# Scores of the local layers in three products instead of four, the mix next to them, and another order of all stages

## The chip, the cores and the metric

One core of one Trainium2 chip. The metric is the device time of one execution in microseconds (us). Three runs of the kernel before took 3424.27, 3425.03 and 3427.98 us; the median is 3425.03. The profile is of one further execution.

## The reference, cut to what matters

A batch of 32 sequences of 128 tokens with 128 features passes four blocks: a cross attention, six local transformer layers, a second cross attention, and a quantised linear layer. The change is in the six local layers only. One layer computes, for 16 heads of width 64:

```python
q, k, v = split(x @ Wqkv)                      # 128 -> 3 * 1024
q = rotary(l2norm(q) * q_scale);  k = rotary(l2norm(k) * k_scale)
# windows of 32 queries; each sees its own 32 keys and the 32 before them
sim  = einsum('bhwie,bhwje->bhwij', bq, bk2) * 8        # masked: later keys, more than 32 back, padding
out  = einsum('bhwij,bhwje->bhwie', softmax(sim), bv2)
x = out @ Wo + x
x = (a * gelu(gate)) @ W2 + b2 + x             # a, gate = split(layernorm(x) @ W1 + b1), width 341 each
```

In front of both halves of a layer the upper 64 features are shifted by one token. All of this is in float32.

## The kernel before, in words

`local_layers` (from line 553 on) writes out the instruction streams of TensorE (`pe`), ScalarE (`act`), VectorE (`dve`), GpSimd (`pool`) and SyncE (`sp`, DMA issues only) by hand. A unit `u` is one sequence in one layer; there are 6 * 32 = 192. Each engine runs a loop over `step`, and in every step it does a fixed list of stages, each for unit `step - lag`; the list and the lags are the order of that engine. Stages that are called `closing` run once in four steps, for a group of four sequences, and `second` ones once in two. The engines are tied by semaphores; an engine does its list strictly in order, so a stage whose input is late holds up everything behind it in the list.

The stages of a unit are, on TensorE: `project` (L732, three times: q, k and v, each two products of 128x512), `transpose_qk` (L742, eight 128x128 transposes each for q and k), `scores` (L759), `mix` (L786), every second step `project_out` (L800), and every fourth step `mlp_mean` (L809), three `mlp_up` (L827), `mlp_variance` (L817) and `mlp_down` (L838). ScalarE squares q and k (L896), takes the reciprocal norms (L905, L907), copies the transposed q and k (`copy_qk`, L914), v (L889) and the mix (L928) out of PSUM and does the exponentials and the gelu, which need different tables. VectorE makes the rotary products (L1026, L1027), the sums of squares (L1034), the mask, the maxima and sums of the softmax and a block transpose of the probabilities. GpSimd does the rest of the rotation (L1154), the normalisation (L1162) and two passes over the probabilities. The transposed probabilities go to DRAM and back (`store_probs`, `place_probs`), and half of v is moved between partitions by DMA (`place_v`).

Each float32 product stands in the profile as two weight loads and two matmuls, which are called records below. A product that needs only a part of the 128x128 array is given a tile of it, by `tile_position` and the size of its operands. In `scores`, for each of the eight pairs of heads (`t`), there are four windows of 32 queries and two heads (`j`, in the upper and the lower 64 rows): 8 products whose weights are 64 rows by 32 columns (64*32 in the profile), with 64 keys moving. That makes 64 products and 128 records for a unit. In `mix` all products have weights of 64*64, and there are 48 products (96 records) for a unit. All the other stages use the whole array (128*128, or 128*85 and 85*128 in the last tile of the MLP).

PSUM is used as four pairs of banks in rotation. The order in which TensorE's stages take them is `ROTATING`, which has to match TensorE's list, and a stage waits until the pair it takes has been read out (`banks.fill`).

Of the kernel before, what the change touches and what calls it, by code (L numbers as in the profile page):

```python
# [17 lines left out]
NB, S, D = 32, 128, 128  # L18
GB = 4
# [6 lines left out]
DEPTH, HD, WIN = 6, 64, 32  # L26
# [19 lines left out]
NEAR = 2 * WIN  # L46
# [72 lines left out]
def build(nc, dram):  # L119
    stack = ExitStack()  # L120
    with stack:
# [34 lines left out]
        def phase_end(engine):  # L156
            engine.drain().then_inc(phase_over, 1)
# [395 lines left out]
        def local_layers(phase):  # L553
            here = ExitStack()
            with here:
# [39 lines left out]
                for n in ("squared", "producted", "summed", "rotations", "normalised", "turned", "copied"))  # L595
# [10 lines left out]
                sem("up_made"), sem("gelu_made"), sem("hidden_made"), sem("down_made"), sem("y_ready"))  # L606

            LAST = 14
            ROTATING = (("q", 0, 1), ("up2", 13, GB), ("mix", 6, 1), ("k", 0, 1), ("v", 4, 1), ("scores", 2, 1), ("out", 6, 2),
                        ("up0", 11, GB), ("mean", 7, GB), ("up1", 11, GB), ("variance", 10, GB), ("down", 13, GB), ("kT", 1, 1),  # L610
                        ("qT", 1, 1))
            pair_of, turn = {}, 0
            for step in range(UNITS + LAST):
                for stage, lag, every in ROTATING:
                    u = step - lag
# [82 lines left out]
            def sp(sp):  # L698
                for step in range(UNITS + LAST):
                    place_probs(step - 5, sp)  # L700
                    layer, into = step // NB, step % NB
                    if layer < DEPTH - 1 and into == NB - 1:
                        load_qk(sp, layer + 1, 1)
                    if 0 < layer < DEPTH and into == 3:
                        load_v(sp, layer)
                    place_v(step - 4, sp)
                    if layer < DEPTH - 1 and into == NB - 2:
                        load_qk(sp, layer + 1, 0)
                    if 0 < layer < DEPTH and into == 5:
                        load_out(sp, layer)  # L710
                    if 0 < layer < DEPTH and into == 12:
                        load_mlp(sp, layer)
                    store_probs(step - 4, sp)
                sp.wait_ge(probs_placed, P_PLACED * UNITS)

            def pe(pe):
# [29 lines left out]
                @each(UNITS)  # L746
                def scores(u):
                    i = pair_of["scores", u]
                    banks.fill(pe, i, (masked, u + 1))
                    pe.wait_ge(copied[0], u + 1)  # L750
                    pe.wait_ge(copied[1], u + 1)
                    for t in range(IT):
                        for window in range(S // WIN):
                            these = slice(window * WIN, (window + 1) * WIN)
                            near = slice(max(window - 1, 0) * WIN, max(window + 1, 2) * WIN)
                            for j in range(2):
                                rows = slice(HD * j, HD * j + HD)
                                at = j * BANK + t * NEAR
                                mm = pe.matmul(  # L759
                                    pairs[i][these, at:at + NEAR], qkT[u % 2][rows, 0, t, these],  # L760
                                    qkT[u % 2][rows, 1, t, near], start=True, stop=True,
                                    tile_position=(rows.start, these.start))
                    mm.then_inc(scored, 1)

                @each(UNITS)
# [74 lines left out]
                    mm.then_inc(down_made, 1)  # L840

                for step in range(UNITS + LAST):
                    project(step, 0)
                    mlp_up(step - 13, 2)
                    mix(step - 6)
                    project(step, 1)
                    project(step - 4, 2)
                    scores(step - 2)
                    project_out(step - 6)
                    mlp_up(step - 11, 0)  # L850
                    mlp_mean(step - 7)
                    mlp_up(step - 11, 1)
                    mlp_variance(step - 10)
                    mlp_down(step - 13)
                    transpose_qk(step - 1, 1)
                    transpose_qk(step - 1, 0)
                phase_end(pe)

            def act(act):
# [122 lines left out]

                for step in range(-1, UNITS + LAST):
                    square(step, 0)
                    reciprocal_norms(step - 1)
                    mlp_gelu(step - 13, 2)
                    mlp_affine(step - 11)
                    mlp_shift(step - 7)
                    square(step, 1)
                    copy_mix(step - 6)  # L990
                    copy_v(step - 4)
                    exponentials(step - 4)
                    prepare(step + 1)
                    mlp_log(step - 10)
                    mlp_root(step - 10)
                    mlp_gelu(step - 11, 0)
                    mlp_gelu(step - 11, 1)
                    mlp_square(step - 9)
                    copy_qk(step - 1, 1)
                    copy_qk(step - 1, 0)  # L1000
                phase_end(act)

            def dve(dve):
# [108 lines left out]
                for step in range(UNITS + LAST):  # L1112
                    if step < UNITS and step % NB == 0:
                        start_layer(step // NB)
                    products(step, 0)
                    turn_probs(step - 5)
                    mlp_hidden(step - 13, 2)
                    products(step, 1)
                    mask_scores(step - 2)
                    sum_squares(step, 0)  # L1120
                    mlp_centre(step - 7)
                    add_out(step - 6)
                    mlp_hidden(step - 11, 0)
                    add_down(step - 13)
                    sum_squares(step, 1)
                    mlp_hidden(step - 11, 1)
                    row_sums(step - 4)
                    clamp_norms(step)
                    row_maxima(step - 2)
                phase_end(dve)  # L1130

            def pool(pool):
                phase_gate(pool, phase)
                for t in (*xs, mlp_xs):
                    pool.memset(t[P // 2:, :, 0:1], 0.0).then_inc(zeroed, 1)

                @each(UNITS)
                def lower(u):
                    pool.wait_ge(maxed, u + 1)
                    pool.tensor_tensor(probs[u % 3][:, :, :], probs[u % 3][:, :, :],  # L1140
                                       negmax[u % 2][:, :].unsqueeze(2).broadcast_to([P, H, NEAR]), ALU.add).then_inc(lowered, 1)

                @each(UNITS)
                def normalise_probs(u):
                    pool.wait_ge(inverted, u + 1)
                    pool.tensor_tensor(probs[u % 3][:, :, :], probs[u % 3][:, :, :],  # L1146
                                       rowsum[u % 2][:, :].unsqueeze(2).broadcast_to([P, H, NEAR]), ALU.mult).then_inc(probs_normed, 1)

                @each(UNITS)
                def rotate(u, part):  # L1150
                    pool.wait_ge(producted[part], u + 1)
                    if u >= 2:
                        pool.wait_ge(turned[part], u - 1)
                    pool.tensor_tensor(rotated[u % 2][:, part].rearrange("p h (s d) -> p s h d", s=2),  # L1154
                                       halves(times_cos[part][:, :]), halves(times_sin[part][:, :]), ALU.add).then_inc(rotations[part], 1)

                @each(UNITS)
                def normalise(u, part):
                    rt = rotated[u % 2][:, part]
                    pool.wait_ge(rnormed, u + 1)  # L1160
                    pool.wait_ge(rotations[part], u + 1)
                    pool.tensor_tensor(rt, rt, rnorm[u % 2][:, part * H:(part + 1) * H].unsqueeze(2).broadcast_to([P, H, HD]),  # L1162
                                       ALU.mult).then_inc(normalised[part], 1)

                @each(UNITS)
                @closing
                def mlp_scale(g):
                    pool.wait_ge(rooted, g + 1)
                    pool.tensor_tensor(centred[:, :], centred[:, :], spread[:, :], ALU.mult).then_inc(scaled, 1)

                for step in range(UNITS + LAST):
                    rotate(step - 1, 1)
                    normalise(step - 1, 1)
                    normalise(step - 1, 0)
                    lower(step - 3)
                    rotate(step, 0)
                    mlp_scale(step - 10)
                    normalise_probs(step - 4)
                phase_end(pool)

            return load_first, sp, pe, act, dve, pool
# [718 lines left out]
```

## Time and profile before

| | |
|---|---|
| median of three runs | 3425.03 us |
| the profiled execution | 3413.21 us, of it span 3411.4 us |
| first attention, until the local layers begin | 0 to about 243 us |
| local layers | about 243 to 3090 us |
| TensorE busy, share of the span | 3245.9 us, 95% |
| VectorE busy | 2943.4 us, 86% |
| GpSimd busy | 2639.8 us, 77% |
| ScalarE busy | 2379.1 us, 70% |
| mean granted TensorE clock | 0.982 of full speed |

"Busy" is the time in which at least one instruction of the engine is under way. The profile shows weight loads (PEld) apart from matmuls (PE); a load normally runs while the matmul before it streams. The start times are what the text reads from; the ends of matmuls are modelled.

### The profile page before, as it was taken

The numbers are of one execution on the slowest core, as the hardware profiler recorded it, in microseconds if no ns is written. First come the engines' busy times: TensorE is split into PE (matmuls) and PEld (weight loads), VectorE is DVE, ScalarE is ACT, GpSimd is POOL, SyncE is SP. The second block draws the span as 40 slices with busy tenths as digits, with TensorE's granted clock in tenths as the row PEclk, the third lists the DMA queues.
The fourth block names the chain that finished last, engine by engine and source line by source line (L and its number), as shares of the span: only waits on it lengthen the run. The fifth ranks groups of instructions, "written<-read, shape, count | busy, mean of one in ns | idle before, by whom it ended". The sixth has DMA issues, their size and how long they took to land.

```text
span 3411.4 us, 130897 instructions
## 1 busy us (share of the span) xinstructions
PE 3245.9 (95%) x56355; PEld 2054.7 (60%) x56386; DVE 2943.4 (86%) x3343; ACT 2379.1 (70%) x4288; POOL 2639.8 (77%) x1408
## 2 busy tenths in 40 slices
PE   7977999999999999999999999999999999977996
PEld 4545666666666666666666666666666666643554
DVE  6869989889999999998989898898999999935887
ACT  6865677667676767676776776776767676746885
POOL 1229988888888888888888888888888888833576
PEclk9989999999999999999999999999999999988998
DMA  2002333443433344334433334343344333330000
GB/s 94 2 1 64 122 113 111 120 126 114 120 112 112 117 126 119 113 108 126 125 113 117 112 110 123 119 120 113 113 125 125 118 111 112 110 123 1 2 11 17
DMA packets 229188, 336.05 MB, mean 99 GB/s; under 512 B 39046, under 2 KB 151044, under 8 KB 228228
## 3 DMA queue, kind: packets, MB, share of 16 engines
q1 hardware_dynamic: 228612, 327.68, 31.7%
q8 instruction: 446, 7.31, 0.9%
q14 instruction: 130, 1.06, 0.1%
HBM read 124.14 MB, written 102.76 MB: 67 GB/s over the span
## 4 chain that ended last, share of the span: by engine, by line
PE 84%; issue 5%; POOL 4%; ACT 3%; DVE 3%; SPq 0%; DMA 0%; POOLq 0%; DVEq 0%; ACTq 0%
PE psum L732 29%; PE psum L800 10%; PE psum L742 9%; PE psum L786 8%; PE psum L759 8%; PE psum L827 7%; PE psum L838 4%; POOL f_rotated L1154 2%; ACT x_expo L1480 1%; PE psum L817 1%; PE psum L809 1%; ACT x_expo L391 1%; PE psum L1337 1%; PE psum L1347 1%; PE psum L309 1%
## 5 line engine op out<-in xcount | busy, mean ns | idle before, releaser
L732 PE MATMUL psum<-w_qkv,f_xs 128*128 128x512 f32 x2304 | 1081.2, 606 | 18.9 <-issue 14.2
L1154 POOL TENSOR_TENSOR f_rotated<-f_times_cos,f_times_sin 128x1024 f32<-128x1024 f32 x384 | 908.7, 2367 | 9.3 <-DVE f_times_sin L1027 9.3
L1162 POOL TENSOR_TENSOR f_rotated<-f_rotated,f_rnorm 128x1024 f32<-128x1024 f32 x384 | 722.6, 1903 | 38.2 <-ACT f_rnorm L907 11.9
L732 PEld LDWEIGHTS psum<-w_qkv,f_xs 128*128 128x128 f32 x2304 | 410.1, 191 | 402.4 <-issue 393.6
L896 ACT ACTIVATE f_squares<-psum 128x1024 f32<-128x1024 f32 x384 | 392.9, 1023 | 361.4 <-PE psum L732 356.4
L1146 POOL TENSOR_TENSOR f_probs<-f_probs,f_rowsum 128x1024 f32<-128x1024 f32 x192 | 365.2, 1902 | 329.1 <-DVE f_rowsum L1066 329.1
L1026 DVE TENSOR_TENSOR f_times_cos<-psum,rot 128x1024 f32<-128x1024 f32 x384 | 469.8, 1223 | 131.6 <-ACT f_squares L896 127.8
L914 ACT COPY f_qkT<-psum 128x1024 f32<-128x1024 f32 x384 | 369.9, 1013 | 210.8 <-PE psum L742 210.7
L1027 DVE TENSOR_TENSOR f_times_sin<-psum,rot 128x1024 f32<-128x1024 f32 x384 | 466.1, 1214 | 0.0
L1034 DVE TENSOR_REDUCE f_sumsq<-f_squares 128x16 f32<-128x1024 f32 x384 | 463.4, 1209 | 0.0
L742 PEld LDWEIGHTS psum<-consts,f_rotated 128*128 128x128 f32 x3072 | 348.5, 141 | 98.0 <-issue 89.2
L742 PE MATMUL psum<-consts,f_rotated 128*128 128x128 f32 x3072 | 371.1, 274 | 17.7 <-POOL f_rotated L1162 14.7
L1140 POOL TENSOR_TENSOR f_probs<-f_probs,f_negmax 128x1024 f32<-128x1024 f32 x192 | 365.2, 1902 | 0.0
L786 PEld LDWEIGHTS psum<-f_probsT,f_v 64*64 64x64 f32 x6144 | 262.9, 135 | 163.1 <-issue 163.1
L800 PE MATMUL psum<-f_outT,w_o 128*128 128x256 f32 x1536 | 358.6, 387 | 1.2 <-ACT f_outT L928 1.2
L759 PEld LDWEIGHTS psum<-f_qkT 64*32 64x32 f32 x24576 | 254.2, 105 | 146.9 <-issue 145.3
L786 PE MATMUL psum<-f_probsT,f_v 64*64 64x64 f32 (+1 forms) x6144 | 310.1, 228 | 15.8 <-issue 15.8
L800 PEld LDWEIGHTS psum<-f_outT,w_o 128*128 128x128 f32 x1536 | 285.1, 190 | 45.5 <-issue 1.8
L786 PE MATMUL psum<-f_probsT,f_v_moved 64*64 64x32 f32 (+1 forms) x12288 | 307.5, 217 | 0.0
L827 PE MATMUL psum<-f_xn,w 128*128 128x512 f32 (+1 forms) x576 | 281.2, 612 | 7.7 <-ACT f_xn L970 7.7
L759 PE MATMUL psum<-f_qkT 64*32 64x64 f32 x24576 | 285.4, 225 | 0.8 <-issue 0.8
L786 PEld LDWEIGHTS psum<-f_probsT,f_v_moved 64*64 64x64 f32 x12288 | 286.2, 136 | 0.0
(175 smaller groups left out, 5159.5 us busy)
## 6 DMA issues: line engine op xcount, KB each, us to landing
f_v_moved<-f_v SPq DMA_DIRECT2D x768, 128.0 KB, 2.8
turned_blocks<-w_qkv SPq DMA_DIRECT2D x192, 512.0 KB, 3.0
f_probsT<-turned_blocks SPq DMA_DIRECT2D x768, 128.0 KB, 2.8
w_qkv<-in_l_wqkv SPq DMA_DIRECT2D x18, 512.0 KB, 4.0
w_o<-in_l_wo SPq DMA_DIRECT2D x6, 512.0 KB, 4.6
w_qkv<-in_ctxT SPq DMA_DIRECT2D x1, 2048.0 KB, 8.7
out<-x_f_result SPq DMA_DIRECT2D x8, 256.0 KB, 2.2
w<-in_l_w SPq DMA_DIRECT2D x6, 341.0 KB
```

Of the source, the lines that this page charges most:

```text
L732: mm = pe.matmul(pairs[i][:, j * BANK:(j + 1) * BANK], xs[g % 2][:, u % GB, :], w_qkv[:, part * INNER + j * BANK:part * INNER + (j + 1) * ...
L742: tr = pe.transpose(pairs[i][:, t * S:(t + 1) * S], rotated[u % 2][:, part, 2 * t:2 * t + 2, :].rearrange("p h d -> p (h d)"), ident)
L759: mm = pe.matmul(pairs[i][these, at:at + NEAR], qkT[u % 2][rows, 0, t, these], qkT[u % 2][rows, 1, t, near], start=True, stop=True, tile_p ...
L786: mm = pe.matmul(pairs[i][cols, at + windows.start * WIN:at + windows.stop * WIN], values, probsT[u % 2][rows, windows, j, :], start=True, ...
L800: mm = pe.matmul(pairs[i][:, 0:GT // 2], w_o[:, t, :], outT[:, t, tokens], start=t == 0, stop=t == IT - 1)
L827: mm = pe.matmul(pairs[i][0:n, a * BANK:a * BANK + GT], w_1[:, a * FF + o:a * FF + o + n], xn[:, :], start=True, stop=True)
L896: act.activation(squares[part][:, :], pair("qk"[part], u), ACT.Square).then_inc(squared[part], 1)
L1026: dve.tensor_tensor(halves(times_cos[part][:, :]), halves(taken), table(0), ALU.mult)
L1027: dve.tensor_tensor(halves(times_sin[part][:, :]), halves(taken)[:, ::-1], table(1), ALU.mult).then_inc(producted[part], 1)
L1034: dve.tensor_reduce(sumsq[u % 2][:, part * H:(part + 1) * H], squares[part][:, :].rearrange("p (s h d) -> p h s d", s=2, h=H), axis=XY, op ...
L1154: pool.tensor_tensor(rotated[u % 2][:, part].rearrange("p h (s d) -> p s h d", s=2), halves(times_cos[part][:, :]), halves(times_sin[part] ...
L1162: pool.tensor_tensor(rt, rt, rnorm[u % 2][:, part * H:(part + 1) * H].unsqueeze(2).broadcast_to([P, H, HD]), ALU.mult).then_inc(normalised ...
```

## The change

Three edits, all in `local_layers`. First, in `scores` the first two windows of a head become one product: 64 queries (weights of 64*64) by the first 64 keys, which are the keys that both windows look at. The other two windows stay as they are (64*32). So there are three products for a head instead of four, 48 in a unit, and 96 records. They are issued pair of heads by pair of heads: two of 64*64, then four of 64*32, then the next pair.

Second, on TensorE `mix` comes directly behind `scores`.

Third, the lists of all engines are in another order, with other lags of v (3 instead of 4), of the exponentials and row sums (3 instead of 4), of lowering by the maxima (2 instead of 3), and of parts of the MLP; `ROTATING` follows.

```diff
-                        for window in range(S // WIN):
-                            these = slice(window * WIN, (window + 1) * WIN)
-                            near = slice(max(window - 1, 0) * WIN, max(window + 1, 2) * WIN)
+                        for these, near in ((slice(0, 2 * WIN), slice(0, 2 * WIN)), (slice(2 * WIN, 3 * WIN), slice(WIN, 3 * WIN)),
+                                            (slice(3 * WIN, 4 * WIN), slice(2 * WIN, 4 * WIN))):
                             for j in range(2):
...
 TensorE:
                 for step in range(UNITS + LAST):
+                    mlp_mean(step - 9)
                     project(step, 0)
-                    mlp_up(step - 13, 2)
+                    mlp_up(step - 12, 2)
+                    scores(step - 2)
                     mix(step - 6)
                     project(step, 1)
-                    project(step - 4, 2)
-                    scores(step - 2)
+                    mlp_up(step - 11, 0)
+                    project(step - 3, 2)
+                    mlp_up(step - 11, 1)
                     project_out(step - 6)
-                    mlp_up(step - 11, 0)
-                    mlp_mean(step - 7)
-                    mlp_up(step - 11, 1)
-                    mlp_variance(step - 10)
                     mlp_down(step - 13)
+                    transpose_qk(step - 1, 0)
                     transpose_qk(step - 1, 1)
-                    transpose_qk(step - 1, 0)
+                    mlp_variance(step - 9)
 ScalarE, after:
                     square(step, 0); mlp_gelu(step - 12, 2); reciprocal_norms(step - 1); copy_mix(step - 6); square(step, 1)
                     exponentials(step - 3); mlp_gelu(step - 11, 0); mlp_affine(step - 10); prepare(step + 1)
                     mlp_square(step - 9); copy_v(step - 3); mlp_gelu(step - 11, 1); copy_qk(step - 1, 0)
                     copy_qk(step - 1, 1); mlp_shift(step - 7); mlp_log(step - 9); mlp_root(step - 9)
 VectorE, after:
                     turn_probs(step - 5); products(step, 0); mlp_hidden(step - 12, 2); sum_squares(step, 0)
                     mask_scores(step - 2); products(step, 1); sum_squares(step, 1); mlp_hidden(step - 11, 0)
                     add_down(step - 13); row_sums(step - 3); add_out(step - 6); mlp_hidden(step - 11, 1)
                     row_maxima(step - 2); mlp_centre(step - 8); clamp_norms(step)
 GpSimd, after:
                     normalise(step - 1, 0); normalise(step - 1, 1); rotate(step, 0); normalise_probs(step - 4)
                     rotate(step, 1); lower(step - 2); mlp_scale(step - 9)
 SyncE:
-                    if 0 < layer < DEPTH and into == 3:
+                    if 0 < layer < DEPTH and into == 2:
                         load_v(sp, layer)
-                    place_v(step - 4, sp)
+                    place_v(step - 3, sp)
```

## Rows read from the trace of the kernel before

**Rows 1.** The page, part 1: busy time and share of each engine.
```profile
PE 3245.9 (95%) x56355; PEld 2054.7 (60%) x56386; DVE 2943.4 (86%) x3343; ACT 2379.1 (70%) x4288; POOL 2639.8 (77%) x1408
```

**Rows 2.** The page, part 4: the chain that ended last, by engine.
```profile
PE 84%; issue 5%; POOL 4%; ACT 3%; DVE 3%; SPq 0%; DMA 0%; POOLq 0%; DVEq 0%; ACTq 0%
```

**Rows 3.** Busy time of each engine in four steps of layer 4.
```profile
core 0: us, PE busy (x) PEld busy (x) DVE busy (x) ACT busy (x) POOL busy (x), PEclk, DMA share, GB/s
1697.13:1754.44 57.31, 57.31 (x1070) 36.63 (x1076) 51.81 (x56) 40.65 (x52) 49.96 (x26) 1.00 0.37 112
```

**Rows 4.** The chain of waits from 1690 to 1760 us: start, duration, what.
```profile
1697.13 1.41 PE psum L759 x91
...
1703.03 1.75 PE psum L742 x16
1704.78 1.72 PE psum L732 x4
1706.50 1.53 PE psum L786 x96
1708.03 3.63 PE psum L732 x8
1711.66 1.42 PE psum L759 x91
...
1754.44 1.42 PE psum L759 x91
```

**Rows 5.** Line 759 between 1705.95 and 1713.2 us: count, shortest/median/longest ns.
```profile
L759 PEld LDWEIGHTS psum<-f_qkT x128: 102/106/107, 1711.6 to 1712.8; 64*32 64x32 f32 x128
L759 PE MATMUL psum<-f_qkT x128: 213/216/240, 1711.6 to 1712.9; 64*32 64x64 f32 x128
```

**Rows 6.** Weight loads around one mix: start us, us, what [idle before].
```profile
1705.05 0.19 PEld L732 LDWEIGHTS psum<-w_qkv,f_xs 128*128 128x128 f32 x1 [0.24 <-issue]
1705.48 0.19 PEld L732 LDWEIGHTS psum<-w_qkv,f_xs 128*128 128x128 f32 x1 [0.24 <-issue]
1706.43 0.13 PEld L786 LDWEIGHTS psum<-f_probsT,f_v 64*64 64x64 f32 x1 [0.76 <-issue]
1706.43 0.13 PEld L786 LDWEIGHTS psum<-f_probsT,f_v_moved 64*64 64x64 f32 x1
1706.44 0.13 PEld L786 LDWEIGHTS psum<-f_probsT,f_v 64*64 64x64 f32 x1
1706.45 0.13 PEld L786 LDWEIGHTS psum<-f_probsT,f_v_moved 64*64 64x64 f32 x1
...
1707.78 0.14 PEld L786 LDWEIGHTS psum<-f_probsT,f_v 64*64 64x64 f32 x1
1707.96 0.30 PEld L732 LDWEIGHTS psum<-w_qkv,f_xs 128*128 128x128 f32 x2
1708.50 0.19 PEld L732 LDWEIGHTS psum<-w_qkv,f_xs 128*128 128x128 f32 x1 [0.24 <-issue]
```

**Rows 7.** Weight loads in the first attention, 118 to 122 us.
```profile
118.14 0.11 PEld L302 LDWEIGHTS psum<-mask_past,ident_bf 128*128 128x128 bf16 x2
118.68 0.97 PEld L309 LDWEIGHTS psum<-x_queries,x_keys 32*128 32x128 f32 x16 [0.42 <-issue]
119.77 0.30 PEld L253 LDWEIGHTS psum<-xres,mean_mat 128*128 128x128 f32 x2
120.83 0.81 PEld L319 LDWEIGHTS psum<-x_expo,x_vpad 128*32 128x32 f32 x32 [0.76 <-issue]
```

**Rows 8.** Transposes, their copies and the q projection behind them, in order of time.
```profile
1716.57 1.91 PE L742 MATMUL psum<-consts,f_rotated 128*128 128x128 f32 x16
1717.64 1.93 ACT L914 COPY f_qkT<-psum 128x1024 f32<-128x1024 f32 x2 [2.75 <-PE psum L742]
1718.31 1.88 PE L732 MATMUL psum<-w_qkv,f_xs 128*128 128x512 f32 x4
```

**Rows 9.** The chain of waits where TensorE takes over, at a layer's start, and after the last q.
```profile
397.46 1.06 PE psum L742 x8
...
1598.95 2.96 issue
1601.91 3.00 PE psum L732 x4
...
2998.49 2.51 issue
```

More of the change, by code:

```diff
@@ L608, in local_layers @@
             LAST = 14
-            ROTATING = (("q", 0, 1), ("up2", 13, GB), ("mix", 6, 1), ("k", 0, 1), ("v", 4, 1), ("scores", 2, 1), ("out", 6, 2),
-                        ("up0", 11, GB), ("mean", 7, GB), ("up1", 11, GB), ("variance", 10, GB), ("down", 13, GB), ("kT", 1, 1),
-                        ("qT", 1, 1))
+            ROTATING = (("mean", 9, GB), ("q", 0, 1), ("up2", 12, GB), ("scores", 2, 1), ("mix", 6, 1), ("k", 0, 1), ("up0", 11, GB),
+                        ("v", 3, 1), ("up1", 11, GB), ("out", 6, 2), ("down", 13, GB), ("qT", 1, 1), ("kT", 1, 1), ("variance", 9, GB))
             pair_of, turn = {}, 0
@@ L758, in scores @@
                                 at = j * BANK + t * NEAR
[L759 to L762, printed above, removed]
+                                mm = pe.matmul(pairs[i][these, at:at + NEAR], qkT[u % 2][rows, 0, t, these],
+                                               qkT[u % 2][rows, 1, t, near], start=True, stop=True,
+                                               tile_position=(rows.start, these.start))
                     mm.then_inc(scored, 1)
@@ L984, in act @@
                     square(step, 0)
+                    mlp_gelu(step - 12, 2)
                     reciprocal_norms(step - 1)
-                    mlp_gelu(step - 13, 2)
-                    mlp_affine(step - 11)
-                    mlp_shift(step - 7)
[L989 to L1000, printed above, removed]
+                    copy_mix(step - 6)
+                    square(step, 1)
+                    exponentials(step - 3)
+                    mlp_gelu(step - 11, 0)
+                    mlp_affine(step - 10)
+                    prepare(step + 1)
+                    mlp_square(step - 9)
+                    copy_v(step - 3)
+                    mlp_gelu(step - 11, 1)
+                    copy_qk(step - 1, 0)
+                    copy_qk(step - 1, 1)
+                    mlp_shift(step - 7)
+                    mlp_log(step - 9)
+                    mlp_root(step - 9)
                 phase_end(act)
@@ L1114, in dve @@
                         start_layer(step // NB)
+                    turn_probs(step - 5)
                     products(step, 0)
-                    turn_probs(step - 5)
-                    mlp_hidden(step - 13, 2)
+                    mlp_hidden(step - 12, 2)
+                    sum_squares(step, 0)
+                    mask_scores(step - 2)
                     products(step, 1)
[L1119 to L1122, printed above, removed]
+                    sum_squares(step, 1)
                     mlp_hidden(step - 11, 0)
                     add_down(step - 13)
-                    sum_squares(step, 1)
+                    row_sums(step - 3)
+                    add_out(step - 6)
                     mlp_hidden(step - 11, 1)
-                    row_sums(step - 4)
+                    row_maxima(step - 2)
+                    mlp_centre(step - 8)
                     clamp_norms(step)
-                    row_maxima(step - 2)
                 phase_end(dve)
@@ L1171, in pool @@
                 for step in range(UNITS + LAST):
-                    rotate(step - 1, 1)
+                    normalise(step - 1, 0)
                     normalise(step - 1, 1)
-                    normalise(step - 1, 0)
-                    lower(step - 3)
                     rotate(step, 0)
-                    mlp_scale(step - 10)
                     normalise_probs(step - 4)
+                    rotate(step, 1)
+                    lower(step - 2)
+                    mlp_scale(step - 9)
                 phase_end(pool)
```

## The prediction

> **What bounds the kernel now.** I read the page's busy shares first: TensorE is at work for 95% of the span, VectorE for 86%, GpSimd for 77% [rows 1]. The chain that ended last, which is where a shorter instruction shortens the run, lies on TensorE for 84% of the span [rows 2]. Then the windows view over four steps of a layer: 57.31 us, of which TensorE is busy for 57.31, VectorE 51.81, GpSimd 49.96 and ScalarE 40.65, with the clock granted in full [rows 3]. So a step takes 14.33 us and TensorE never rests; if it were faster, the next floors would be VectorE at 51.81 / 4 = 12.95 us a step and GpSimd at 12.49. The chain view of the same stretch says what a step is made of: transposes 1.75, q 1.72, mix 1.53, k and v 3.63, scores 1.42, and one MLP or output stage, here 3.65 [rows 4]. The reader is to see that each piece begins where the last one ends. The chain is of this kind from 398.5 us, where GpSimd stops being the last, to 2998.5 us; in between lie five starts of a layer, where it shows a wait of 2.96 us and a slow first q of 3.00 instead of 1.72, some 5 us each with what follows [rows 9]. (2600 - 25) / 14.33 = 180 steps are set by TensorE, and each is worth what TensorE gains or loses in it.
>
> **What a change of tile costs on TensorE.** This decides the case, so I read it from the weight loads. Inside a run of full-array products a load starts 0.43 us after the one before (1705.05, 1705.48), as soon as the earlier matmul begins to stream: it is hidden. The next load, the first of `mix` with 64*64, would be due at 1705.91. It starts at 1706.43, that is when the last full product, begun at 1705.91 and streaming 0.43, has ended, and 0.09 later [rows 6]. Within `mix` four tiles load at 1706.43 to .45, about 7 ns apart, beside each other. On the way out the last load is at 1707.78 and the first full one only at 1707.96, and its product streams only when that load is through, 0.30 - 0.19 = 0.11 us later [rows 6]. The first attention shows the same with rows alone cut (128*128 to 32*128: the two full loads are over at 118.25, and the next, at 118.68, has waited 0.42 us for their products) and with columns alone cut (128*128 to 128*32: second stream from 119.77 + 0.11 + 0.43 = 120.31 to 120.74, load at 120.83, 0.09 later) [rows 7]. So each change of the tile's shape that this trace has empties the array: about 0.09 us after the last stream, and then a weight load that nothing hides. It has no change between two cut shapes, and the new `scores` makes fifteen of them in a unit: 64*64, 64*32, 64*64, and so on through the eight pairs of heads.
>
> The Trainium skill, "TensorEngine Tiling (Array Packing)", Tiling Modes, says that changing the tiling mode, and not just the tile, drains TensorE. The rows above agree for changes from and to the full array; for 64*64 to 64*32 no row shows it. By the page my forecast holds, and without it the first rival would be as good.
>
> **Part 1, three products for a head.** Removed: 128 - 96 = 32 records in a unit. Now 128 records take 1.42 us [rows 4, 5], 11.1 ns each. If only their number counts, 96 take 1.07 and the unit gains 0.35 us. If each change of shape empties the array, a pair of heads takes two legs, one after the other:
> - 64*64, two tiles side by side, two records in each. A full load and a full stream of 128 columns take 1.75 / 16 = 0.109 us [rows 4], so 64 columns take 0.053. Load 0.053, two streams 0.107, empty 0.09: 0.25 us.
> - 64*32, four tiles, two records in each: load 0.027, two streams 0.107, the last tile's first record six places behind (at 7 to 11 ns, 0.04 to 0.07), empty 0.09: 0.26 to 0.29 us.
>
> Together 0.51 to 0.54 us, times eight 4.1 to 4.3; I take 4.2. Against 1.42 that is +2.78 us a step. Ends for this unknown: below, no emptying, 1.07 (-0.35); above, every leg waits for the whole recorded matmul of 0.216 us [rows 5] in place of its stream, 0.32 + 0.37 a pair, 5.5 us (+4.1). I stand near the lower part of the emptying case because the three changes seen all give 0.09 to 0.10 after the stream, not after the record.
>
> **Part 2, mix behind scores.** Two q or k and v stages between cut shapes show the price of a visit to the full array: k and v together take 3.63 us between `mix` and `scores`, where four records take 1.72 and eight would take 3.44 [rows 4]. The 0.19 is the exposed load of 0.11 and the emptying of 0.09. One such visit goes away in each step: -0.19. The change from 64*32 to the 64*64 of `mix` stays, and its emptying is in the last leg above. If the array does not empty there, the gain is the same to within 0.1 us.
>
> **Part 3, the order and the lags.** No instruction is added or taken; they move.
> - `scores` had q, mix, k and v between it and the transposes (1.72 + 1.53 + 3.63); now in the leanest steps only q. The two copies of the transposes end at 1717.64 + 1.93 = 1719.57, and TensorE would reach `scores` at 1718.31 + 1.72 = 1720.03 [rows 8]. Some 0.4 us is left, so I cost it at nothing. If ScalarE comes late by more, everything on TensorE is late by the rest, since `mix` and k are queued behind.
> - `mix` comes 1.42 us or so later after `turn_probs` and the DRAM round trip than before, which helps. v is made and moved one step earlier: `place_v`, four DMAs on SyncE's queue, stands before `store_probs` as before, with one more step until `mix`. `load_v` moves with it. Both at nothing, covered by a whole step; uncovered, a DMA's landing would cost some us once a layer.
> - `mlp_centre` now waits on VectorE for `mlp_mean` at the head of TensorE's next step, once in four steps. Behind it stand `clamp_norms` and the next `turn_probs`; ScalarE needs the clamped sums only behind its square of the next q, which itself needs 1.72 us of TensorE. Nothing. In the same way `mlp_log` on ScalarE and `mlp_scale` on GpSimd wait for a variance at TensorE's step end; behind them stand a square that waits for q in any case, and `normalise`. Nothing.
> - `lower` follows `row_maxima` in the same step instead of the next. VectorE has 14.33 - 12.95 and GpSimd 14.33 - 12.49 us of slack a step [rows 3], and more if TensorE gets longer. Bounds for the whole order: -0.1 us a step (nothing on TensorE stalls now, so hardly below nothing) and +1.4, VectorE's whole slack turned into a stall.
>
> **The sum.** 14.33 + 2.78 - 0.19 = 16.92 us a step; 2.59 * 180 = +466 us. Span 3411.4 + 466 = 3877, execution +1.8 = 3879. The profiled execution of before lies 11.8 us below the median of its runs; with that, 3891 us.
>
> **The rivals.**
> - *Faster: no emptying between the two cut shapes.* They need not conflict, since 64*64 sits in the first 64 columns and the two 64*32 in the last 64, and tiles of one shape do run beside each other [rows 6]. Against it: a full load does run ahead of a full product on the very same cells, so what holds the load back at each change is not that the cells are in use, but the change. Then a step gains 0.35 + 0.19 = 0.54, 180 * 0.54 = 97: 3328 us. If the 96 records go at the pace of `mix`, 1.53 / 96 = 15.9 ns [rows 4], `scores` takes 1.53 and the whole gives 0.08 a step, 14 us: 3411. It is decided at an internal change costing (0.35 + 0.19) / 15 = 0.04 us: above that the kernel is slower. 0.04 is less than half of the 0.09 alone.
> - *Half an emptying.* Between two cut shapes the array may be empty in half the time, 0.045 us, with the next load partly beside it: legs of 0.20 and 0.22, `scores` 3.4, +1.79 a step, +322: 3747 us. The way out of `mix` speaks against it, where the first full load is as late as after a full product.
> - *No emptying, and the order is late.* `scores` stands 0.4 us behind its input, VectorE 0.8 us a step from its floor. A stall of 0.5 to 0.8 us a step takes back the 0.54: 3420 to 3470 us.
>
> **How the numbers follow.** Full emptying 0.60, with 3800 to 3980 us as its own range (legs shorter by the overlap of a load, or 0.4 us more a step from each engine's waits and the emptying at 0.12); half or less, 3500 to 3800, 0.08; above 3980, 0.03; no emptying 0.24, between 3320 and 3411; late order 0.05. The likeliest is 3891. To leave out no more than 2 in 10 the range has to reach over to the fast case: 3325 to 3980. A measurement of this kernel tells a change from none at about 0.2%, 7 us. Slower by more: 0.60 + 0.08 + 0.03 + 0.04 of the late order = 0.75, less 0.03 for small costs in the case between: 0.72. Faster 0.24, within 0.2% 0.04.
>
> **What the profile after would show.** If I am right: line 759 has 18432 matmuls, its time in the chain is about 4.2 us a step, the weight loads in it show a pause before each leg, VectorE's share falls to about 76%, and TensorE's idle time in front of 759's loads grows by over 2 us a unit. If the rival is right: 759 takes 1.1 us in the chain, a step 13.8 us, VectorE at 94%. In both, the full-array stages should show 0.19 less between cut shapes. A chain that leaves TensorE in the steady steps, for ScalarE's copies above all, would show that the order is the cause. Wrong would be: one record rate throughout line 759 without pauses.

## The result and the profile after

The changed kernel takes 3834.28 us (median of 4 runs, 3832.24 to 3840.2) against 3424.65 us for the kernel before (median of 4): a ratio of 1.12, with a 95% interval of 1.1183 to 1.1217. It is 12% slower. The forecast was 3891 us. Its range of 3325 to 3980 reached over to a faster kernel; 3800 to 3980 was the part of it for full emptying at every change. The profiled execution took 3832.62 us, its span 3830.8, so 419.4 us more than the 3411.4 of before.

The page, parts 1 and 4, and from part 5 the group of the scores (now line 757; 731 is the projections, 741 the transposes, 783 `mix`, 797 the output projection, 824 and 835 the MLP):

```profile
PE 3705.9 (97%) x50211; PEld 2352.0 (61%) x50242; DVE 2934.8 (77%) x3343; ACT 2271.0 (59%) x4196; POOL 2641.5 (69%) x1408
...
PE 89%; issue 4%; DVE 3%; ACT 3%; POOL 1%; SPq 0%; DMA 0%; POOLq 0%; DVEq 0%; ACTq 0%
PE psum L731 26%; PE psum L757 20%; PE psum L741 9%; PE psum L797 9%; PE psum L783 8%; PE psum L824 6%; PE psum L835 3%; ACT x_expo L1477 1%; PE psum L814 1%; PE psum L806 1%; ACT x_expo L391 1%; PE psum L1334 1%; PE psum L1344 1%; PE psum L309 1%; DVE x_negmax L472 1%
...
L757 PE MATMUL psum<-f_qkT 64*32 64x64 f32 (+1 forms) x18432 | 793.0, 233 | 1.5 <-ACT f_qkT L911 1.4
```

Against [rows 1] VectorE's and GpSimd's busy time has not changed (2934.8 and 2641.5 us), only their share of a longer span. TensorE has 6,144 matmuls fewer and is busy for 460 us more. The scores were 8% of the chain and are 20%.

Four steps of the middle of a layer, windows view and chain of waits (start, duration, what), which answer to [rows 3] and [rows 4]:

```profile
1909.09:1976.19 67.10, 67.10 (x936) 42.89 (x938) 52.01 (x55) 38.34 (x49) 49.98 (x26) 1.00 0.34 103
```

```profile
1905.62 1.75 PE psum L741 x16
1907.37 1.72 PE psum L731 x4
1909.09 4.06 PE psum L757 x96
1913.15 1.53 PE psum L783 x96
1914.68 1.92 PE psum L731 x4
...
1936.15 3.45 PE psum L797 x16
1939.60 1.75 PE psum L741 x16
...
1976.19 4.06 PE psum L757 x96
```

A step is 67.10 / 4 = 16.78 us where it was 14.33, at the same full clock, and TensorE still never rests. The scores take 4.06 us instead of 1.42: +2.64. `mix` is 1.53 as before. The output projection, which came directly behind the scores in [rows 4], now stands between full stages and takes 3.45 instead of 3.65. 2.64 - 0.19 = 2.45 a step.

The scores of one unit, shortest/median/longest ns (answers to [rows 5]), and two slices of 0.05 us, one from each of two successive legs, of line 757 alone (columns: PE, then PEld, busy and count, granted clock, DMA share, GB/s):

```profile
L757 PEld LDWEIGHTS psum<-f_qkT x96: 102/106/133, 1909.0 to 1912.9; 64*32 64x32 f32 x64, 64*64 64x64 f32 x32
L757 PE MATMUL psum<-f_qkT x96: 215/229/268, 1909.0 to 1912.9; 64*32 64x64 f32 x64, 64*64 64x64 f32 x32
```

```profile
1927.31:1927.36 0.05, 0.05 (x8) 0.00 (x0) 1.00 0.60 246
...
1927.56:1927.61 0.05, 0.05 (x4) 0.00 (x0) 1.00 0.80 328
```

A single record is as short as before. What has grown is the distance: in each leg of about 0.25 us there is a slice with matmuls in flight and no weight load at all. The shares of busy time hide this, since records of 0.22 us bridge the pauses; the number of records and the length of the stage show it.

### The profile page after: what moved, and what is told of

Read it like the earlier page. It is cut to its first block, busy times and chain, and to the rows that moved or that the text cites. A ratio compares the mean times of both kernels' runs of the same rounds, so it can differ in the third digit from the quotient of the medians.

```text
span 3830.8 us, 118517 instructions
## 1 busy us (share of the span) xinstructions
PE 3705.9 (97%) x50211; PEld 2352.0 (61%) x50242; DVE 2934.8 (77%) x3343; ACT 2271.0 (59%) x4196; POOL 2641.5 (69%) x1408
## 4 chain that ended last, share of the span: by engine, by line
PE 89%; issue 4%; DVE 3%; ACT 3%; POOL 1%; SPq 0%; DMA 0%; POOLq 0%; DVEq 0%; ACTq 0%
PE psum L731 26%; PE psum L757 20%; PE psum L741 9%; PE psum L797 9%; PE psum L783 8%; PE psum L824 6%; PE psum L835 3%; ACT x_expo L1477 1%; PE psum L814 1%; PE psum L806 1%; ACT x_expo L391 1%; PE psum L1334 1%; PE psum L1344 1%; PE psum L309 1%; DVE x_negmax L472 1%
## 5 line engine op out<-in xcount | busy, mean ns | idle before, releaser
L757 PE MATMUL psum<-f_qkT 64*32 64x64 f32 (+1 forms) x18432 | 793.0, 233 | 1.5 <-ACT f_qkT L911 1.4
L757 PEld LDWEIGHTS psum<-f_qkT 64*32 64x32 f32 (+1 forms) x18432 | 536.5, 113 | 374.4 <-issue 147.9
L925 ACT COPY f_outT<-psum 128x1024 f32<-128x1024 f32 x192 | 194.3, 1012 | 759.5 <-PE psum L783 759.5
L797 PEld LDWEIGHTS psum<-f_outT,w_o 128*128 128x128 f32 x1536 | 295.0, 192 | 82.8 <-issue 46.2
```

Of the source, the lines that this page charges most:

```text
L757: mm = pe.matmul(pairs[i][these, at:at + NEAR], qkT[u % 2][rows, 0, t, these], qkT[u % 2][rows, 1, t, near], start=True, stop=True, tile_p ...
L797: mm = pe.matmul(pairs[i][:, 0:GT // 2], w_o[:, t, :], outT[:, t, tokens], start=t == 0, stop=t == IT - 1)
```

## Experiments

Ratios are to the kernel before on the same chip, with 95% intervals; before ran there at 3415 to 3417 us (beside the changed kernel: 3424.65).

### The products alone

```diff
 # kernel before, its order kept; in scores:
-                        for window in range(S // WIN):
-                            these = slice(window * WIN, (window + 1) * WIN)
-                            near = slice(max(window - 1, 0) * WIN, max(window + 1, 2) * WIN)
+                        for these, near in ((slice(0, 2 * WIN), slice(0, 2 * WIN)), (slice(2 * WIN, 3 * WIN), slice(WIN, 3 * WIN)),
+                                            (slice(3 * WIN, 4 * WIN), slice(2 * WIN, 4 * WIN))):
```

> The kernel before with only the scores changed to three products a head; order and lags of before. Emptying theory: scores take 4.06 us as in the changed kernel, +2.64 a step, 180 steps +475, less up to 25 us at the layer starts: 3875 to 3900 us (ratio 1.13 to 1.14). Rival (the order is to blame for the loss): under 3500 us.

Measured: 3889.41 us, ratio 1.1388 (1.1366 to 1.1409). A scores stage begins at 2005.87 and the next stage at 2009.92: 4.05 us. As expected; the products bring the whole loss, and more than the whole change does. Beside them, order and lags are worth 1.1388 - 1.12 = 0.0188, 64 us in the kernel's favour. The mix behind the scores explains 0.195 * 180 = 35 of them; the rest was not taken apart.

### How much one change of shape costs: 15, 7, 3, 1 and none

Three kernels have the same products as the changed kernel, but issue the 64*64 ones of a group of pairs first and then their 64*32 ones, in groups of 2, 4 and 8 pairs (changed kernel: 1).

```diff
-                    for t in range(IT):
-                        for these, near in (...):
+                    wide = ((slice(0, 2 * WIN), slice(0, 2 * WIN)),)
+                    narrow = ((slice(2 * WIN, 3 * WIN), slice(WIN, 3 * WIN)), (slice(3 * WIN, 4 * WIN), slice(2 * WIN, 4 * WIN)))
+                    for first in range(0, IT, 8):             # 2 and 4 in the others
+                        for leg in (wide, narrow):
+                            for t in range(first, first + 8):
+                                for these, near in leg:
```

> The changed kernel with the scores grouped by shape over two pairs of heads: seven changes of shape inside the stage in place of fifteen. From the two ends measured, 4.06 us with fifteen and 2.11 with one, a change costs 1.95 / 14 = 0.139 us, so the stage takes 2.11 + 6 * 0.139 = 2.94 us. If it is not the changes but the place of the products that counts, it need not lie on that line.

> The same over four pairs of heads: three changes of shape. By the line 2.11 + 2 * 0.139 = 2.39 us for the stage. By the theory of supply, scores and mix are 384 records in 2.39 + 1.53 = 3.92 us, so TensorE stops in mix in some steps as with one change, though for less.

> The changed kernel with the scores' products grouped by shape: the sixteen of 64*64 for all eight pairs of heads first, then the 32 of 64*32. One change of shape inside the stage in place of fifteen, same products. Emptying alone: 4.06 less 14 changes at 0.13 to 0.14 us gives 2.1 to 2.2 us. If the array could use all its tiles in both groups it would be 96 records at 11.1 ns, 1.07, plus one change, 1.2 us. Second theory, that a tile takes one record in 0.058 us (the pace of mix: 0.350 us for six records of a tile in a pair of heads) and each group here has only a half of the tiles: 16 * 0.058 * 2 = 1.87 plus two legs' loads and emptying 0.27 = 2.1 us. Step 14.14 + 0.7 = 14.85; 3410 + 130 - 20 = about 3515 us (ratio 1.027). Rival without the second theory: 3360 us.

The fourth makes all products of the scores 64*64, so that there is no change of shape at all, not even towards `mix`:

```diff
-                        ... (slice(2 * WIN, 3 * WIN), slice(WIN, 3 * WIN)),
-                            (slice(3 * WIN, 4 * WIN), slice(2 * WIN, 4 * WIN))):
+                        ... (slice(2 * WIN, 4 * WIN), slice(WIN, 3 * WIN)),
+                            (slice(2 * WIN, 4 * WIN), slice(2 * WIN, 4 * WIN))):
```

> The changed kernel with all products of the scores of 64*64: the third and fourth window are each made by a product of queries 64 to 127, both written to the same place, so the third window's scores are taken against the fourth window's keys; everything else is unchanged. Still 96 records, 48 products, but no change of shape inside the stage. Emptying theory with a tile's pace of 0.058 us: the tiles of the upper columns take 32 records each, 1.87 us, plus 0.14: 2.0 us, step 14.7, about 3500 us. If only the number of records counts, 96 at mix's 15.9 ns: 1.53 us, about 3410 us. If emptying had no part in the loss, the stage would stay near 4 us and the time near 3834 us.

The scores stage in the chain of waits of each, in this order (groups of 2, 4, 8, all 64*64):

```profile
1923.70 2.94 PE psum L760 x96
```

```profile
1916.42 2.38 PE psum L760 x96
```

```profile
1925.42 2.11 PE psum L760 x96
```

```profile
1924.26 1.85 PE psum L757 x78
1926.11 0.05 PE psum L783
1926.16 0.06 PE psum L757 x2
...
1927.45 0.65 issue
...
1939.09 1.85 PE psum L757 x78
...
1941.09 1.40 PE psum L783 x70
1942.48 1.91 PE psum L731 x4
```

| changes of shape inside the stage | stage, us | kernel, us | ratio (95%) |
|---|---|---|---|
| 15 (changed kernel) | 4.06 | 3834.28 | 1.12 (1.1183 to 1.1217) |
| 7 | 2.94 | 3661.97 | 1.0715 (1.0677 to 1.0752) |
| 3 | 2.38 | 3598.63 | 1.0529 (1.049 to 1.0568) |
| 1 | 2.11 | 3571.89 | 1.0457 (1.0436 to 1.0478) |
| none, all 64*64 | 1.85, until `mix` takes over in the chain | 3534.44 | 1.0362 (1.0336 to 1.0389) |

The first four rows lie on a straight line: (4.06 - 2.11) / 14 = 0.139 us for each change, and 0.14 for each step between the rows. So the price is per change. In the last row the first records of `mix`, which have the same shape, begin between the last ones of the scores: without a change two stages overlap. There the two stages have to be taken together: 3.39 us (1939.09 to 1942.48) against 2.11 + 1.53 = 3.64 with one change inside. Two changes have gone, that inside and that towards `mix`, and 0.25 us with them, so this kernel lies near the same line. The Trainium skill, "TensorEngine Tiling (Array Packing)", Tiling Modes, says that a change of the tiling mode drains TensorE; these runs agree, now between two cut shapes as well, and 0.139 us is its price here.

With one change left the stage is still 0.69 us longer than the 1.42 of before, though it has 32 matmuls fewer. 0.14 is that change. The other 0.55 I put down to each shape using one half of the array's columns: the first leg runs in two tiles, the second in four, 16 matmuls in each tile and the legs one after the other. In the kernel with 64*64 alone the two busiest tiles get 32 matmuls each, and 1.85 / 32 = 0.058 us a matmul; two legs of 16 at this pace are 1.86 us, near the 1.97 that the line gives for no change. Before, the 64*32 form spread 128 matmuls over eight tiles, 16 in each, all at once: 1.42 us. Fewer matmuls in fewer tiles are not less time.

Two whole kernels had a forecast, and both came out above it: 3571.89 us against about 3515 with one change, 3534.44 against about 3500 with none. The chain shows a wait inside `mix` behind the shorter stage (the `issue` in the last fence; 1.89 us in one step of the kernel with groups of 8). In the whole run TensorE waits for `issue` in front of `mix` for 6.6 us with 15 changes, 25.8 with 7, 55.7 with 3, 69.6 with 1 and 78.0 with none: the shorter the scores, the longer the wait. That is the subject of the next runs.

### The order alone

The changed kernel with the old 64*32 products put back (the diff of the first experiment, reversed).

> The changed kernel with the four-window scores of before put back: only the order and the lags are new. Emptying theory: scores back to 1.42 us a step, and the visit to the full array that is saved stays saved, so a steady step is 14.33 - 0.19 = 14.14 us, 180 steps give -34 us, and the time is about 3390 us (ratio 0.990). If TensorE's gaps at the five layer starts were hidden only by the longer step, they come back. Rival (the new order costs something itself): 3425 us or more, with a chain that leaves TensorE in the steady steps.

Measured: 3743.13 us, ratio 1.0967 (1.0941 to 1.0993). My theory (3390) failed by 350 us; the rival had the sign and the size was beyond both. The scores stage is 1.41 us, as it was. The chain:

```profile
1923.62 1.41 PE psum L758 x91
1925.03 0.97 PE psum L785 x55
1926.00 2.99 issue
1928.99 1.29 PE psum L785 x41
1930.28 4.74 PE psum L731 x8
```

and the windows of the stop and of what follows it (PE, PEld, DVE, ACT, POOL, clock, DMA share, GB/s), with the longest waits of TensorE in the whole run:

```profile
1926.00:1928.99 2.99, 0.00 (x0) 0.00 (x0) 2.99 (x3) 0.00 (x0) 2.99 (x2) 1.00 0.24 70
1928.99:1935.01 6.02, 6.02 (x50) 3.43 (x50) 0.96 (x2) 2.69 (x3) 4.68 (x3) 0.72 0.19 60
```

```profile
PE psum L785 <- issue: 231.3, 135, 4.0
PE psum L758 <- issue: 25.5, 26, 2.0
```

TensorE stops in the middle of `mix`, after 55 of its records, for 2.99 us, waiting for no other engine. Behind the stop the granted clock is 0.72 over 6.02 us, a mean between its two levels (1.2 and 2.4 GHz), and k and v take 4.74 us instead of 3.63. The place of the stop is not fixed in the program's loops: in successive steps it came after 62, 55, 41, 29 and 12 matmul records of `mix`. With all of TensorE's instructions counted alike, which adds some 8 semaphore instructions a step to the loads and matmuls, five successive stops are exactly 512 apart (58560, 59072, 59584, 60096, 60608; a step has some 536 loads and matmuls, [rows 3], which makes the drift).

That number has a meaning in part 3 of the page. The queue `instruction` moves blocks of 16 KB. It moves 446 of them here and in the kernel before, and 398 in the changed kernel, which has 6,144 matmuls and as many loads fewer: 12,288 / 48 = 256 records a block. So TensorE stops at every second boundary between blocks, the one that falls into `mix`. The queue's rows (queue, blocks, MB, share):

```profile
q8 instruction: 446, 7.31, 0.8%
```

One block begins to move at 1926.61, 2.4 us before TensorE goes on. The packets of this queue and TensorE's instructions, counted over the run, make the link firmer. Before the blocks that begin to move at 1926.61, 1943.08 and 1960.48 there had been 231, 233 and 235 of them, and the stops at 59584, 60096 and 60608 are each 448 above 256 times that number: TensorE stands still where what has been moved is used up. Of the 140 stops over 0.8 us in these two stages 136 lie a multiple of 256 instructions apart. In 2.95 us the two stages behind each other use up 448 records, which is 1.75 blocks, where a whole step of 14.33 us needs 2.1. I read this as TensorE running out of instructions: for a short while it is faster than the queue. A block does not move more slowly than before: between 1900 and 2000 us each takes 0.88 to 1.35 us, and 0.93 to 1.32 between 1690 and 1790 in the kernel before. The boundaries and the moving blocks are what the trace shows; how the queue decides when to fetch it does not.

In sum: TensorE is busy for 127 us more than before (3372.8 against 3245.9; the mean granted clock is 0.952 against 0.982) and sits idle for `issue` in these two lines for 240 us more (256.8 against the 16.6 of before). That makes 367 us, against 349 more of span.

### The same with k between scores and mix

```diff
 # order alone, and in the steps of TensorE and ScalarE:
+                    k(step - 0)
                     mix(step - 6)
-                    k(step - 0)
```

(shortened to the two calls that change places; the copies that follow them move alike.)

> The order-only kernel (four windows, new order) with the k projection put between scores and mix, on TensorE, in the rotation of the PSUM pairs and in ScalarE's list. The order-only kernel lost 328 us although no engine's work grew; its TensorE stops in the middle of mix, waiting for nothing that the profile shows, and these stops lie exactly 512 TensorE records apart (records 59072, 59584, 60096, 60608), while the queue that brings instructions moves blocks of 16 KB, about 256 records each. Theory of supply: scores and mix back to back are 448 records in 2.95 us, and the next block is not there yet; 1.72 us of k between them, 8 records, lets it come. Then the stops go and the time is 3400 to 3440 us. Rival (a lag or another engine's place in the new order is the cause): it stays near 3740 us.

Measured: 3455.7 us, ratio 1.0108 (1.0085 to 1.0132), some 15 us above the expected end. Chain of waits:

```profile
1937.43 1.41 PE psum L758 x91
1938.84 1.91 PE psum L731 x4
1940.76 1.53 PE psum L785 x96
1942.29 1.91 PE psum L731 x4
...
1954.45 1.80 PE psum L785 x84
```

The k projection, four matmuls of 512 columns, between the two bursts brings back 287 of the 328 us, with the same number of instructions and the same lags. The visit to the full array costs its 0.19 us again, and that is by far the cheaper. Some stops stay (28.7 us before line 785, 32.1 before 758), which accounts for the miss.

### Each product of the scores twice

```diff
 # kernel before:
-                    for t in range(IT):
+                    for t in (t for t in range(IT) for twice in range(2)):
```

> The kernel before with every product of the scores issued twice in a row, same tiles, same places. No shape changes inside, the order of before. Work alone: +1.42 us a step, 180 steps, +256: 3680 us. Theory of supply: 512 records without a pause in 2.84 us are one more than the store of two blocks can hold ahead, so TensorE stops in the stage in each step, for 1.5 to 2.5 us: 3900 to 4150 us, with stops 512 records apart. If the rate of the stage was itself set by the tiles, the second product of a tile adds its full 0.107 us: no more than 3700.

Measured: 4188.6 us, ratio 1.2251 (1.2204 to 1.2298), above what either theory named. The added work alone is 1.42 * 180 = 256 us, which would give 3673. TensorE waits for `issue` in this stage for 364.2 us in all, 179 times, and the mean granted clock is 0.953; the forecast had no term for the clock. The timeline of one such stage:

```profile
1921.27 2.54 PE L759 MATMUL psum<-f_qkT 64*32 64x64 f32 x238
1925.65 0.41 PE L759 MATMUL psum<-f_qkT 64*32 64x64 f32 x18 [1.85 <-issue]
```

A burst of 512 records (256 loads and 256 matmuls) in the order of before, with no cut stage next to it, is enough for a stop of about 2 us. Here the stops lie 768 instructions apart (76705, 77473, 78241, 79009): three blocks, and a step has 536 + 256 = 792 loads and matmuls. The count of blocks fits as well: 638 against 446 is 192 more, for 49,152 records more, again 256 in each. So neither the new order nor `mix` is at fault, but the number of small records in a stretch.

The Trainium skill, "Runtime: NRT & Kernel Launch", Instruction fetch mechanics, says that instructions come in blocks of 16 KiB, 256 instructions each; the counts agree. It also says that the fetch is hidden by the rate of issue. The stops disagree, and they decide: the kernel with the new order alone lost 240 us in them.

### Another order of the same products

```diff
 # kernel before:
-                        for window in range(S // WIN):
+                        for j, window in ((j, window) for j in range(2) for window in range(S // WIN)):
```

> The kernel before with the two inner loops of the scores exchanged: all four windows of one head, then of the other, same 64 products of 64*32. The stage now takes 11.1 ns a record, though a tile's two records need only 0.107 us of the 0.178 us of a pair of heads. If the rate is that of handing out instructions, the order is indifferent: 3425 us, ratio 1.000. If neighbours in other rows overlap better than neighbours in other columns, it is slower: each record 13 ns or more, stage 1.7 us, 3475 us.

Measured: 3416.94 us, ratio 0.9998 (0.9985 to 1.0011). With one shape throughout, it does not matter in which order neighbouring records visit the tiles; what mattered above was the shape, not the tile's place.

### The start of a layer

The layers are 461.7 to 465.1 us apart before, and 32 steps of 14.33 are 458.6. The stop of [rows 9] follows a load that SyncE issues late. SyncE's own rows in the kernel before:

```profile
1594.63 1.83 SPq L688 DMA_DIRECT2D f_probsT<-turned_blocks  x4
1596.51 0.43 SPq L628 DMA_DIRECT2D w_qkv<-in_l_wqkv  x1
```

The load at 1596.51 is that of the next layer's k weights. It stands behind `place_probs`, which waits for the DRAM round trip, and the first q of the layer waits for one semaphore that counts the loads of q and k together. The experiment puts this load ahead of `place_probs`:

```diff
 # kernel before, SyncE's step:
+                    if layer < DEPTH - 1 and into == NB - 1:
+                        load_qk(sp, layer + 1, 1)
                     place_probs(step - 5, sp)
-                    if layer < DEPTH - 1 and into == NB - 1:
-                        load_qk(sp, layer + 1, 1)
```

> The kernel before with one edit on SyncE: in the last step of a layer the load of the next layer's k weights and scales is issued ahead of place_probs, not behind it. In the kernel before it is issued at 1596.51 us, after place_probs at 1594.63, though k of the last unit was projected by 1590.4; VectorE and TensorE then stand at the layer's start for about 5 us. Theory: the load lands 4 to 6 us earlier and the five gaps of about 5 us go: 3400 us, ratio 0.993. Rival (the gap has another cause): 3425 us, ratio 1.000.

```profile
1585.23 0.43 SPq L628 DMA_DIRECT2D w_qkv<-in_l_wqkv  x1
...
1587.89 2.56 SPq L688 DMA_DIRECT2D f_probsT<-turned_blocks  x4
```

```profile
1590.29 1.91 PE L742 MATMUL psum<-consts,f_rotated 128*128 128x128 f32 x16
1592.04 1.88 PE L732 MATMUL psum<-w_qkv,f_xs 128*128 128x512 f32 x4
```

Measured: 3399.65 us, ratio 0.9949 (0.9929 to 0.9969): the one version that beats both kernels. The first q of the layer follows the transposes at once and takes its normal time, and layers are 460.0 to 460.3 us apart.

## Why the prediction was right

**What bounds the kernel.** Right. TensorE sets each step before and after, from about 310 us on in the changed kernel.

**Changes of the tile's shape.** Right, and it was the step that decided. The threshold was 0.04 us per change; it is 0.139. The threshold itself rested on 1.07 us for the products without a change, and that is wrong too, as the low end below. My two legs came to 0.51 to 0.54 us for a pair of heads, the measured pair is 4.06 / 8 = 0.507. Its parts: 15 * 0.139 / 8 = 0.26 for the changes and 1.97 / 8 = 0.246 for the matmuls, where 1.97 is the stage extrapolated to no change. Of the two ends I gave, neither the 1.07 (no emptying) nor the 5.5 us (a leg waits for the recorded matmul) is near. The low end was wrong in itself: without emptying the 96 matmuls take 1.85 to 1.97 us, not 1.07, since each shape keeps only half of the tiles at work. The first rival's 3328 us did not exist; even then the stage would have lost 0.4 us or more.

**Mix behind scores.** Right as far as the stages go: 0.195 us a step, from the MLP and output pieces of four steps (16.36 us in all against 17.14), where 0.19 was forecast. The sentence that the gain "is the same" if the array does not empty is not borne out: in the kernel of 64*64 alone nothing empties there, and the stops in front of `mix` come to 78.0 / 180 = 0.43 us a step. With the short scores of before, the new order costs 1.8 us a step (328 / 180), most of it with `mix` right behind them. The slow scores of this change are what keeps the instructions coming: of stops inside `mix` the changed kernel has 6.6 us in all.

**Order and lags at nothing.** Right within the changed kernel, wrong as a general statement. The waits that I went through (the copies before scores, `mlp_mean`, the variances, `lower`) hardly show up, the copies with 1.4 us in the whole run, but I looked only for waits on other engines. That the order costs nothing here is luck in one respect: the forecast did not ask whether instructions arrive in time, and the slow scores cover it. What the order costs with other products, 1.8 us a step, lies above my bound of 1.4 and in a resource that I had not named.

**The sum.** Forecast 3891, measured 3834.28, 57 too high. Three causes explain most of it: the step is 16.78 and not 16.92, 0.14 * 180 = 25 us. The five layer starts are nearly gone, covered by the longer step: layers are 537.6 to 538.3 us apart, and 32 * 16.78 is 537.0; a gap of some 4.8 us became one of 1, five times 3.8 = 19. The run of the products alone shows that it is the step and not the new order: with the order of before and a step of 16.97 its layers are 545.0 us apart, and 32 * 16.97 is 543.0. And the profiled execution now lies 1.7 us below the median where I had carried over 11.8: 10 us. Counted the other way, 2.45 * 180 - 19 = 422, and the spans differ by 419.4.

**Signs in the profile.** 18432 matmuls, pauses at each leg and VectorE at 77% came as named. "Idle time in front of 757's loads grows by over 2 us a unit" did not: together with that in front of `mix` it grew from 310 to 403 us, 0.5 a unit, because the overlapping records of the loads cover the pauses.

## What to carry to other kernels

Read a change of the tile's shape on TensorE as an item with a price, here 0.14 us, and count the changes before the records; products of one shape that keep all tiles at work beat fewer products in two shapes. Keep bursts of small matmuls apart: two cut stages of 128 and 96 matmuls cost 0.2 us a step with four large matmuls in between (3455.7 against 3417.32 us), and 1.8 us without them. And look at what a DMA stands behind on its queue: one load moved ahead of a wait brought 0.5%, where the rewrite of the stage lost 12%.

## What the runs showed that I had not expected

- TensorE can wait for its own instructions: stops of mostly 1 to 3 us with no releaser, a multiple of 256 instructions apart (512 in one kernel, 768 in another), where 384 to 512 small records follow each other. In the chain they stand as `issue`.
- A stop can have a tail. After 2.99 us of rest the granted clock was 0.72 over the next 6.02 us, and 3.63 us of products took 4.74. After the stop of 1.45 us at 1944.10 the clock stayed at its upper level; what decides it was not tested.
- A change between 64*64 and 64*32 costs 0.139 us, though the two shapes lie in different columns of the array.
- Stages of one shape run into each other: the first records of `mix` began 0.16 us before the last one of the scores (1911.28 and 1911.44), in the kernel where both are 64*64.
